# A feed-forward over four experts, computed by sorted slots of one expert each

## The chip, the cores and the metric

The kernel runs on one core of one Trainium2 chip. The metric is the device time of one execution in microseconds (us); the time given is the median of 3 runs.

## The reference

Two layers act on x of shape (2, 2048, 128), float32. Attention has 16 heads of width 8, a causal window of 128 tokens, and a latent branch over 64 pooled rows, mixed by a gate. It is kept as it is. The feed-forward picks one of four experts for each token:

```python
x = x + _layernorm(attention(_layernorm(x)))
x = x + _layernorm(ffn(_layernorm(x)))

# ffn, on x of 4096 tokens, H = 128, I = 512, E = 4
logits = x @ W_router
expert_idx = jnp.argmax(logits, axis=-1)
h = jnp.einsum('th,ehi->tei', x, W1) + b1
h = jax.nn.gelu(h, approximate=False)
onehot = jax.nn.one_hot(expert_idx, E, dtype=x.dtype)
intermediate = jnp.einsum('te,tei->ti', onehot, h)
y = intermediate @ Wo + bo + x
y = _layer_norm(y, ln_gamma, ln_beta)
```

## The kernel before

Tokens lie in 32 tiles of 128 (NB), which make 8 chunks of 512 (NCH, four tiles each, CT). The program has three parts, each a block that every engine leaves before the next begins.

`project` norms x, makes q, k and v and writes q and k to DRAM in three bfloat16 parts. `attend` goes over the tiles in steps s = -2 to 34 (`schedule`). In step s each engine does, in eight groups g = 0 to 7, a piece of the score maxima of tile s + 2, the probabilities and values of tile s, and the gate, output product and norming of tiles s - 1 to s - 3. So the last three steps, 32 to 34, only drain. The order on each engine is written out by hand: PE scores, products and transposes; DVE maxima (L1097) and small row operations, with `ystats`, `yve`, `ybias` for the norming of tile s - 3; ACT exponentials (L1325) and the norming `yn` (L1376); POOL the causal clearing of probabilities (L1242, L1245), the power `yrstd` (L1270), gate arithmetic, and last the addition of `yn` to X (L1311). In steps 30 and 31 DVE also splits the biases b1 into three bfloat16 parts (L1107 to L1125) and makes the low part of W1 (L1129). SP issues the loads. Where PE would pause, bfloat16 products of a constant tile fill the time (`keep_warm`, L124, and `beside`).

`InputNorm` norms the 512 rows of one chunk for the feed-forward: statistics and aggregate on DVE (L197, L201), epsilon and power on POOL (L206, L209), four subtract-and-multiply operations on DVE (L215).

`ffn` goes over the chunks, a straight start, a hardware loop and a straight end. A chunk is transposed (PE, L1531), split in a high and a low fp32r part, and its logits are made (L1542). DVE turns them into a one-hot row with five small operations (L1640 to L1650), which PE transposes and spreads over the partitions, one expert at a time (L1521). DVE multiplies the high and the low part by each expert's row (L1689, L1690), so that a token's columns are zero for three experts. PE then sums over all four experts for each quarter j of I:

```python
def hidden(c, j, e):
    for k, (w, x) in enumerate(((w1hi, xehi), (w1lo, xehi), (w1hi, xelo))):
        nc.tensor.matmul(psH[j % 2][:], w[:, e, tile], x[:, u, e], ...)
```

That is 48 matmuls of 512 columns in a chunk (L1510), and one for the bias of each quarter (L1513). ACT applies Gelu (L1769), PE multiplies by Wo (L1553, 16 matmuls that stand as 32 in the profile). The rest stands one and two chunks later: DVE adds the input (L1675), statistics (L1598, L1602), the norming (L1697); POOL gamma and beta (L1752, L1756); then DVE a second norming (L1610), the residual (L1615), and SP stores the chunk in one DMA (L1489).

## Time and profile before

| | |
|---|---|
| median of 3 runs | 551.62 us (549.55 to 555.9) |
| the profiled execution | 553.63 us |
| its span, first to last instruction | 551.8 us |
| mean granted TensorE clock | 0.955 |
| busy: PE, DVE, ACT, POOL | 506.1, 428.4, 297.2, 326.9 us |
| attention begins, ends | about 85, 367 us |
| feed-forward | 367 to 552 us |

Times in the profile count from the span's start. PE is the matmul engine and PEld its weight loads, DVE the vector, ACT the scalar, POOL the GpSimd engine, SP the one that issues DMAs here (SPq is its queue). A row names line, engine, operation, output<-inputs. A duration of an instruction runs from its start to its end and may overlap with the next one's, so the spacing of two starts is what one costs in a row.

### The profile page before, as it was taken

The numbers are of one execution on the slowest core, as the hardware profiler recorded it, in microseconds if no ns is written. First come the engines' busy times: TensorE is split into PE (matmuls) and PEld (weight loads), VectorE is DVE, ScalarE is ACT, GpSimd is POOL, SyncE is SP. The second block draws the span as 40 slices with busy tenths as digits, with TensorE's granted clock in tenths as the row PEclk, the third lists the DMA queues.
The fourth block names the chain that finished last, engine by engine and source line by source line (L and its number), as shares of the span: only waits on it lengthen the run. The fifth ranks groups of instructions, "written<-read, shape, count | busy, mean of one in ns | idle before, by whom it ended". The sixth has DMA issues, their size and how long they took to land. (4 is left out here: it accounts for less than half of the span.)

```text
span 551.8 us, 16727 instructions
## 1 busy us (share of the span) xinstructions
PE 506.1 (92%) x5277; PEld 312.0 (57%) x5280; DVE 428.4 (78%) x2018; ACT 297.2 (54%) x820; POOL 326.9 (59%) x735
## 2 busy tenths in 40 slices
PE   8978579999999999999999999869999999999991
PEld 3434224565666565565665665535677577677671
DVE  5986586899999999999999898635657677685655
ACT  2655305788888888788888888512211211312110
POOL 4799302688888888588888789841113333333241
PEclk9999855999999999999999999988999999999996
DMA  4465460324213323222332000000000000000001
GB/s 127 132 221 174 150 109 2 100 66 97 46 32 61 83 63 64 45 36 64 64 64 58 10 4 4 2 1 0 1 1 1 21 20 0 19 20 0 20 19 39
DMA packets 49059, 28.10 MB, mean 51 GB/s; under 512 B 6808, under 2 KB 48056, under 8 KB 48976
## 3 DMA queue, kind: packets, MB, share of 16 engines
q1 hardware_dynamic: 47648, 26.73, 19.7%
q8 instruction: 41, 0.67, 0.5%
q10 hardware_dynamic: 1328, 0.36, 0.3%
q14 instruction: 42, 0.34, 0.2%
HBM read 17.90 MB, written 8.91 MB: 49 GB/s over the span
## 5 line engine op out<-in xcount | busy, mean ns | idle before, releaser
L1097 DVE CUSTOM_DVE_ANT_0 added<-psS,maskq 128x256 bf16<-128x256 f32 x512 | 199.8, 415 | 25.4 <-PE psS L938 18.5
L1325 ACT ACTIVATE probs<-psST 128x512 f32<-128x512 f32 x240 | 143.4, 598 | 37.5 <-PE psST L974 35.3
L974 PE MATMUL psST<-qst,kst 50*128 50x128 bf16 x992 | 101.1, 222 | 0.0
L938 PE MATMUL psS<-kst,qst 48*128 48x256 bf16 x448 | 91.7, 287 | 2.3 <-DVE rowmax L1097 1.3
L1769 ACT ACTIVATE hT<-fpsH 128x512 f32<-128x512 f32 x32 | 19.2, 599 | 121.6 <-PE fpsH L1513 121.6
L995 PE MATMUL psPV<-probs,vst 128*10 128x128 f32 x1984 | 80.1, 277 | 3.1 <-issue 0.6
L1242 POOL TENSOR_SCALAR_AFFINE_SELECT probs<-probs 128x256 f32<-128x256 f32 x150 | 62.0, 414 | 5.2 <-ACT probs L1325 5.0
L1245 POOL TENSOR_SCALAR_AFFINE_SELECT probs<-probs 128x256 f32<-128x256 f32 x150 | 62.6, 417 | 0.0
L938 PEld LDWEIGHTS psS<-kst,qst 48*128 48x128 bf16 x448 | 25.2, 95 | 62.4 <-issue 39.5
L974 PEld LDWEIGHTS psST<-qst,kst 50*128 50x128 bf16 x992 | 55.9, 95 | 0.0
L1510 PE MATMUL fpsH<-xehi,w1hi 128*128 128x512 f32 x128 | 55.7, 435 | 0.0
L995 PEld LDWEIGHTS psPV<-probs,vst 128*10 128x10 f32 x1984 | 43.4, 91 | 16.0 <-issue 5.7
L1510 PE MATMUL fpsH<-xelo,w1hi 128*128 128x512 f32 x128 | 50.6, 395 | 0.0
L1510 PE MATMUL fpsH<-xehi,w1lo 128*128 128x512 f32 x128 | 50.5, 395 | 0.0
L1097 DVE DVE_READ_ACCUMULATOR2_ANT rowmax<- 128x1 f32 x512 | 42.6, 83 | 0.0
L962 PE MATMUL psST<-maskk,identb 128*128 128x512 bf16 (+1 forms) x106 | 40.1, 378 | 0.0
L1752 POOL TENSOR_TENSOR y<-y,gamma 128x512 f32<-128x512 f32 x7 | 9.1, 1293 | 52.1 <-DVE y L1697 52.1
L1364 ACT ACTIVATE lexp<-psA,lmin 128x64 f32<-128x64 f32 (+1 forms) x128 | 37.1, 300 | 0.0
L1689 DVE TENSOR_TENSOR xehi<-fpsE,xfThi 128x512 fp32r<-128x512 f32 x32 | 22.0, 688 | 19.3 <-PE fpsE L1521 9.7
L1553 PE MATMUL fpsY<-wo,hT 128*128 128x128 f32 x256 | 30.6, 278 | 0.7 <-ACT hT L1769 0.7
L1510 PEld LDWEIGHTS fpsH<-xehi,w1hi 128*128 128x128 f32 x128 | 24.0, 188 | 11.9 <-issue 8.4
L1553 PEld LDWEIGHTS fpsY<-wo,hT 128*128 128x128 f32 x256 | 29.2, 192 | 1.2 <-ACT hT L1769 1.0
(198 smaller groups left out, 1078.8 us busy)
## 6 DMA issues: line engine op xcount, KB each, us to landing
q_parts<-early SPq DMA_DIRECT2D x8, 384.0 KB, 2.6
k_parts<-early SPq DMA_DIRECT2D x8, 384.0 KB, 2.7
qst<-q_parts SPq DMA_DIRECT2D x32, 96.0 KB
kst<-k_parts SPq DMA_DIRECT2D x32, 96.0 KB
X<-in_L_attn_x_dram SPq DMA_DIRECT2D x8, 256.0 KB, 3.2
qst<-q_parts SPq DMA_DIRECT2D x32, 64.0 KB
kst<-k_parts SPq DMA_DIRECT2D x32, 64.0 KB
out_dram<-res SPq DMA_DIRECT2D x8, 256.0 KB, 2.3
```

The costliest lines, as they stand in the source:

```text
L938: last = nc.tensor.matmul(bank[:, a], q, kst[rows, slot, ring(n - 1, 2)], start=True, stop=True)
L962: nc.tensor.matmul(psST[g % 2][:].rearrange("p a (s q) -> p a s q", s=2)[:, :, sides[0]:2], identb[:], maskk[:, sides[0]:2].unsqueeze(1).b ...
L974: last = nc.tensor.matmul(bank[:, a, side * P:(side + 1) * P], kst[rows, slot, ring(n - 1 + side)], qst[rows, slot, ring(n)], start=not ma ...
L995: last = nc.tensor.matmul(psPV[32 * t:32 * t + VW, G * P:(G + 1) * P], vst[:, n.k - 1 + side, SLOTS * (t // 2) + 2 * G + a, :], probs[:, u ...
L1097: taken = nc.vector.tensor_tensor_reduce(added[:, 2 * (g % 2) + a], psS[g % 2][:, a], mask, 1.0, NEG * 4, ALU.add, ALU.max, rowmax[:, n.mo ...
L1242: nc.gpsimd.affine_select(out=before, in_=before, compare_op=ALU.is_gt, fill=0.0, base=0, pattern=[[0, 2], [1 - P, P]], channel_multiplier=P)
L1245: nc.gpsimd.affine_select(out=own, in_=own, compare_op=ALU.is_gt, fill=0.0, base=0, pattern=[[0, 2], [1, P]], channel_multiplier=-1).then_ ...
L1325: nc.scalar.activation(probs[:, g ^ 1], psST[g % 2][:].rearrange("p a c -> p (a c)"), ACT.Exp, scale=SCALE).then_inc(s_exp.sem, 1)
L1364: nc.scalar.activation(per_lat(lexp, s)[:, h], per_lat(psA, s)[:, h], ACT.Exp, bias=lmin[:, s.mod(2), h:h + 1], scale=-1.0, accum_out=lsum ...
L1510: nc.tensor.matmul(psH[j % 2][:], w[:, e, tile], x[:, u, e], start=(e == 0 and k == 0), stop=False)
L1553: last = nc.tensor.matmul(psY[:, t * P:(t + 1) * P], hT[:, m.mod(2), j, t * P:(t + 1) * P], wo[:, j], start=(j == 0), stop=(j == IT - 1))
L1689: nc.vector.tensor_tensor(xehi[:, u, e], psE[e % 2][:], xfThi[:, u].bitcast(F32), ALU.mult)
```

## The change

Each token goes through its own expert only. Three things are new.

First, routing. `Route` takes one chunk: four transposes and a copy (`turned`, `copied`), logits, the choice (six small DVE operations, now with a signed one-hot), ranks of the tokens among those of their expert (eight small bfloat16 matmuls with a triangle and with ones), places (five small DVE operations, with a running count `following`), and `move`: four indirect DMAs, issued on POOL, that scatter 128 rows of 1028 bytes each (normed row, row, token number) to a DRAM buffer `by_expert`. Chunks 0 to 4 are routed in steps 30 to 34 of attention, chunks 5 to 7 at the head of `ffn`. The buffer holds two pairs of experts, each filled from both ends, and is blanked before by 19 stores on ACT's queue in steps 3 to 21.

Second, slots. DVE maps 11 slots of 512 rows (8 + 4 - 1) to experts and places, 23 small operations. Slots beyond those used read a blank one, so 11 are always computed. SP reads expert and place of each slot into registers and loads the slot's rows and weights, six and three deep. PE does 12 expert matmuls of 512 columns for a slot instead of 48 for a chunk. The bias is added by Gelu.

Third, the steps of a slot stand over four iterations: PE transposes n + 1, multiplies n, and makes the output of n - 1. ACT does both normings, four operations each, with bias and scale tiles; DVE does gamma and beta and the sums; POOL the two powers and four indirect stores of 128 rows. The nine operations on b1 leave DVE. In steps 30 and 31 only two groups of eight keep their `beside` fillers. The first norming writes into a tile `rows`, which also holds the row itself in place of X. `project` gets some 37 small memsets and an iota.

```diff
+SLOT = CH
+NS = NCH + E - 1
+TILE_RING = 6
+W_RING = 3
+ROUTED = 5
+ROUTE_FROM = NB - 2
...
+    def turned(self, pe, c, bank):
+        nc, norm = self.nc, self.norm
+        pe.wait_ge(norm.s_xf.sem, norm.s_xf.after(c))
+        pe.wait_ge(self.s_rTc.sem, self.s_rTc.after(c - 1))
+        for t in range(CT):
+            last = nc.tensor.transpose(bank[:, t * P:(t + 1) * P], self.held.rows[:, c.times(CT, t), 0:D], self.ident[:])
+        last.then_inc(self.s_rT.sem, 1)
...
+    def logits(self, pe, c, bank):
+        u = c.mod(2)
+        pe.wait_ge(self.s_rTc.sem, self.s_rTc.after(c))
+        pe.wait_ge(self.s_place.sem, self.s_place.after(c - 1))
+        for t in range(CT):
+            last = self.nc.tensor.matmul(bank[:, t * E:(t + 1) * E], self.xfT[:, u, t * P:(t + 1) * P], self.held.wr[:],
+                                         start=True, stop=True)
+        last.then_inc(self.s_logit.sem, 1)
...
+    def ranks(self, pe, c, bank):
+        nc, ones = self.nc, self.filler[:, 0:P]
+        pe.wait_ge(self.s_oh.sem, self.s_oh.after(c))
+        pe.wait_ge(self.s_place.sem, self.s_place.after(c - 1))
+        flat = self.signed[:].rearrange("p t e -> p (t e)")
+        nc.tensor.matmul(bank[:, 0:CT * E], self.held.tri[:], flat, start=True, stop=False)
+        for t in range(1, CT):
+            nc.tensor.matmul(bank[:, t * E:CT * E], ones, flat[:, 0:(CT - t) * E], start=False, stop=(t == CT - 1))
+        for t in range(CT):
+            last = nc.tensor.matmul(bank[:, CT * E:(CT + 1) * E], ones, self.signed[:, t],
+                                    start=(t == 0), stop=(t == CT - 1))
+        last.then_inc(self.s_rank.sem, 1)
...
+    def move(self, pool, c):
+        if c.k == 0:
+            pool.wait_ge(self.s_blank, 16 * (SPARE + 1))
+        pool.wait_ge(self.s_place.sem, self.s_place.after(c))
+        pool.wait_ge(self.norm.s_xf.sem, self.norm.s_xf.after(c))
+        for t in range(c.times(CT), c.times(CT, CT)):
+            self.nc.gpsimd.indirect_dma_start(self.by_expert,
+                                              bass.IndirectOffsetOnAxis(ap=self.where[:, t:t + 1], axis=0),
+                                              self.held.rows[:, t], None, bounds_check=2 * PAIR_ROWS - 1,
+                                              oob_is_err=False).then_inc(self.s_moved, 16)
...
+        def routed(s, lead=0):
+
+            c = s.k - ROUTE_FROM + lead
+            return chunk(c) if 0 <= c < ROUTED + lead else None
...
+                            if not (s + 2).live and g in (0, 6):
+                                beside(bankT, g % 2, 2 * P)
...
+                    if g == 2 and routed(s):
+                        route.turned(pe, routed(s), bankT)
+                    if g == 4 and routed(s):
+                        route.logits(pe, routed(s), bankR)
+                    if g == 6 and routed(s):
+                        route.ranks(pe, routed(s), bankP)
...
+                    if (g, a) == (0, 1) and routed(s, 1):
+                        c = routed(s, 1)
+                        dve.wait_ge(s_x1.sem, s_x1.after(step(0, CT * c.k + CT - 1)))
+                        norm.statistics(dve, c)
+                    if (g, a) == (1, 0) and routed(s):
+                        norm.apply(dve, routed(s))
+                    if (g, a) == (5, 1) and routed(s):
+                        route.choose(dve, routed(s), bankR)
+                    if (g, a) == (7, 1) and routed(s):
+                        route.places(dve, routed(s), bankP)
...
+                if routed(s, 1):
+                    norm.deviations(pool, routed(s, 1))
...
+                if routed(s):
+                    route.move(pool, routed(s))
...
+                    if g == 7 and 3 <= s.k < 3 + SPARE + 1:
+                        block = s.k - 3
+                        act.dma_start(by_expert[block * SLOT:(block + 1) * SLOT].rearrange("(t p) w -> p t w", p=P),
+                                      held.blank[:].unsqueeze(1).broadcast_to([P, CT, ROW])).then_inc(s_blank, 16)
...
+            sp.wait_ge(s_map, MAPPED)
+            for i in range(W_RING):
+                load_weights(i)
...
+            sp.wait_ge(route.s_moved, 16 * NB)
+            for i in range(W_RING):
+                load_tile(i)
+            for i in range(W_RING, NS):
+                load_tile(i)
+                load_weights(i)
...
+            for c in range(ROUTED, NCH):
+                route.ranks(pe, chunk(c), psP[:])
+                if c + 1 < NCH:
+                    route.turned(pe, chunk(c + 1), psT[0][:])
+                    route.logits(pe, chunk(c + 1), psR[:])
+                keep_warm(nc, psY[1][:], filler, 5)
+            keep_warm(nc, psY[1][:], filler, 24)
...
-                for k, (w, x) in enumerate(((w1hi, xehi), (w1lo, xehi), (w1hi, xelo))):
-                    nc.tensor.matmul(psH[j % 2][:], w[:, e, tile], x[:, u, e], start=(e == 0 and k == 0),
-                                     stop=False)
-                if e == E - 1:
-                    nc.tensor.matmul(psH[j % 2][:], b1p[:, j * P:(j + 1) * P], onehotT[:, u], start=False,
-                                     stop=True).then_inc(s_h.sem, 1)
...
+                for k, (w, x) in enumerate(((0, xhi), (1, xhi), (0, xlo))):
+                    last = nc.tensor.matmul(psH[j % 2][:], w1[:, r, w, cols], x[:, u], start=(k == 0), stop=(k == 2))
+                last.then_inc(s_h.sem, 1)
...
+            for i in range(-1, NS + 1):
+                n = nth_slot(i)
+                if (n + 1).live:
+                    transposed(n + 1)
                 if n.live:
...
+                    hidden(n, 0)
+                    hidden(n, 1)
+                if (n - 1).live:
+                    outputs(n - 1)
...
                 if n.live:
...
+                    hidden(n, 2)
+                    hidden(n, 3)
...
+            norm.apply(dve, chunk(ROUTED))
+            for c in range(ROUTED, NCH):
+                route.choose(dve, chunk(c), psR[:])
+                if c + 1 < NCH:
+                    norm.statistics(dve, chunk(c + 1))
+                route.places(dve, chunk(c), psP[:])
+                if c + 1 < NCH:
+                    norm.apply(dve, chunk(c + 1))
...
+            for i in range(-1, NS + 3):
+                n = nth_slot(i)
+                if (n - 3).live:
+                    shift(s_sh3, s_rs3, n - 3, mv3, rstd3, shift3)
+                if (n + 1).live:
+                    low(n + 1)
+                if (n - 2).live:
+                    shift(s_sh2, s_rs2, n - 2, mv2, rstd2, shift2)
+                if (n - 3).live:
+                    result(n - 3)
+                if (n - 2).live:
+                    affine(n - 2)
+                if (n - 1).live:
+                    summed(n - 1)
...
+            def normed(n):
+                u = n.mod(2)
+                act.wait_ge(s_sh2.sem, s_sh2.after(n))
+                act.wait_ge(s_y4.sem, s_y4.after(n - 2, 1))
+                for t in range(CT):
+                    last = nc.scalar.activation(y2[:, u, t], y1[:, u, t], ACT.Identity, bias=shift2[:, u, t:t + 1],
+                                                scale=rstd2[:, u, t:t + 1])
+                last.then_inc(s_y2.sem, 1)
...
+            for i in range(0, NS + 3):
+                n = nth_slot(i)
+                if (n - 2).live:
+                    deviations(s_st2, s_rs2, s_y2, n - 2, ve2, rstd2)
+                if (n - 3).live:
+                    store(n - 3, range(CT - 1))
+                if (n - 2).live:
+                    deviations(s_st3, s_rs3, s_y5, n - 2, ve3, rstd3)
+                if (n - 3).live:
+                    store(n - 3, range(CT - 1, CT))
```

On POOL, the drain of attention, steps 32 to 34. Names: `yrstd` the power for a tile's norming, `gdiff`, `mixed` and `diff` the gate, `X` or `rows` the residual row, `rstd` the power of `InputNorm`. Before:

```order
L1270 TENSOR_TENSOR yrstd<-yve,mhalf 128x1
L1280 TENSOR_TENSOR gdiff<-diff,gate 128x128
L1285 TENSOR_TENSOR mixed<-gdiff,both 128x128
L1297 TENSOR_TENSOR diff<-both 128x144
L1311 TENSOR_TENSOR X<-X,yn 128x128
L206 TENSOR_TENSOR ve<-mv,eps_col 128x4
L209 TENSOR_TENSOR rstd<-ve,mhalf 128x4
L1270 TENSOR_TENSOR yrstd<-yve,mhalf 128x1
```

And after the change, from the end of step 31:

```order
L1449 TENSOR_TENSOR rows<-X,yn 128x128
L297 DMA by_expert<-rows,where 9728x257 x4
L334 TENSOR_TENSOR rstd<-ve,mhalf 128x4
L1408 TENSOR_TENSOR yrstd<-yve,mhalf 128x1
L1418 TENSOR_TENSOR gdiff<-diff,gate 128x128
L1423 TENSOR_TENSOR mixed<-gdiff,both 128x128
L1435 TENSOR_TENSOR diff<-both 128x144
L1449 TENSOR_TENSOR rows<-X,yn 128x128
L297 DMA by_expert<-rows,where 9728x257 x4
L334 TENSOR_TENSOR rstd<-ve,mhalf 128x4
L1408 TENSOR_TENSOR yrstd<-yve,mhalf 128x1
```

Four indirect DMAs and the power of the next chunk now stand between a step's residual row and the next step's `yrstd`.

On ACT, one chunk of the feed-forward's straight start before. `xfT` and `xfThi` are the transposed chunk and its high part, `onehotT` the choice, `hT` the Gelu:

```order
L1777 ACTIVATE xfT<-fpsT 128x512
L1779 ACTIVATE xfThi<-xfT 128x512
L1769 ACTIVATE hT<-fpsH 128x512 x2
L1786 ACTIVATE onehotT<-fpsO 12x512
L1769 ACTIVATE hT<-fpsH 128x512 x2
```

And one slot after (L1944 is the second norming, of slot n - 3, L1935 the first, of n - 2):

```order
L1921 ACTIVATE xhi<-fpsT 128x512
L1944 ACTIVATE y<-y,shift,rstd 128x128 x4
L1927 ACTIVATE hT<-fpsH,bias 128x512 x2
L1935 ACTIVATE y<-y,shift,rstd 128x128 x4
L1927 ACTIVATE hT<-fpsH,bias 128x512 x2
```

The two normings, DVE's before, stand ahead of and between the Gelus.

On DVE, one slot after. `xlo` is the low part, `shift` minus mean times the power, `res` the row to be stored:

```order
L1820 SCALAR_TENSOR_TENSOR shift<-mv,rstd 128x4
L1826 TENSOR_TENSOR xlo<-fpsT,xhi 128x512
L1820 SCALAR_TENSOR_TENSOR shift<-mv,rstd 128x4
L1845 TENSOR_TENSOR res<-y,tile 128x512
L1831 TENSOR_TENSOR y<-y,gamma 128x512
L1835 TENSOR_TENSOR y<-y,beta 128x512
L1809 BN_STATS fstats<-y 128x6 x4
L1813 BN_AGGR mv<-fstats 128x2 x4
L1815 TENSOR_SCALAR ve<-mv 128x4
L1851 TENSOR_TENSOR y<-fpsY,tile 128x512
L1855 TENSOR_TENSOR y<-y,bob 128x512
L1809 BN_STATS fstats<-y 128x6 x4
```

The affine part of slot n - 2, which waits for ACT's norming, stands ahead of the sum of slot n - 1, whose output PE has made.

## Rows read from the trace of the kernel before

**Rows 1.** Busy time by stage: length, PE, PEld, DVE, ACT, POOL, granted clock, DMA share, GB/s.
```profile
85.00:366.00 281.00, 268.83 (x4113) 162.90 (x4113) 248.51 (x1383) 228.48 (x705) 223.78 (x585) 0.97 0.22 47
...
409.00:540.00 131.00, 130.22 (x670) 92.16 (x667) 85.85 (x300) 25.32 (x43) 44.80 (x54) 1.00 0.05 15
```

**Rows 2.** The chain that ended last, one chunk: start, length, what.
```profile
457.95 0.59 PE fpsT L1531 x4
458.54 2.80 PE fpsH L1510 x12
...
461.66 0.98 PE fpsR L1542 x8
462.64 3.68 PE fpsY L1553 x32
```

**Rows 3.** Groups by line and form: busy us, mean ns of one, idle before.
```profile
L1675 DVE TENSOR_TENSOR y<-fpsY,XF 128x512 f32<-128x512 f32 x8 | 5.5, 690 | 5.5 <-PE fpsY L1553 5.5
...
L1729 POOL TENSOR_TENSOR rstd<-ve,mhalf 128x4 f32<-128x4 f32 x16 | 16.2, 1014 | 1.3
...
L1769 ACT ACTIVATE hT<-fpsH 128x512 f32<-128x512 f32 x32 | 19.2, 599 | 121.6 <-PE fpsH L1513 121.6
...
L1376 ACT ACTIVATE yn<-y,ybias,yrstd 128x128 f32<-128x128 f32 x32 | 16.0, 501 | 4.2 <-DVE ybias L1164 4.2
...
L654 ACT ACTIVATE early<-psQ,bq 128x512 bf16<-128x512 f32 x8 | 5.5, 684 | 7.8 <-DMA rq_t<-early 6.5 <-PE psQ L706 1.3
```

**Rows 4.** DVE in order of time: start, length, operation, idle time before it.
```profile
372.30 0.17 DVE L1642 TENSOR_TENSOR iseq<-fpsR,lmx 128x16 f32<-128x16 f32 x1
372.50 0.17 DVE L1645 TENSOR_TENSOR rank<-iseq,prio 128x16 f32<-128x16 f32 x1
...
447.08 0.87 DVE L1598 BATCH_NORM_STATS2 fstats<-y 128x6 f32<-128x128 f32 x4
448.11 0.38 DVE L1602 BATCH_NORM_AGGREGATE mv<-fstats 128x2 f32<-128x6 f32 x4 [0.15 <-DVE fstats L1598]
449.70 1.12 DVE L1610 TENSOR_SCALAR y<-y,mv,rstd 128x128 f32<-128x128 f32 x4 [1.22 <-POOL rstd L1729]
```

**Rows 5.** POOL in order of time, steps 30 and 31.
```profile
343.27 0.94 POOL L1242 TENSOR_SCALAR_AFFINE_SELECT probs<-probs 128x256 f32<-128x256 f32 x1
...
352.69 0.41 POOL L1245 TENSOR_SCALAR_AFFINE_SELECT probs<-probs 128x256 f32<-128x256 f32 x1
```

**Rows 6.** All engines in order of time, from attention into the feed-forward.
```profile
357.43 3.19 PE L124 MATMUL psS<-filler 128*128 128x512 bf16 x14
...
362.83 0.46 POOL L1311 TENSOR_TENSOR X<-X,yn 128x128 f32<-128x128 f32 x1 [2.40 <-ACT yn L1376]
...
366.38 0.45 POOL L1311 TENSOR_TENSOR X<-X,yn 128x128 f32<-128x128 f32 x1 [1.32 <-ACT yn L1376]
367.62 1.27 POOL L1739 TENSOR_TENSOR XF<-xf,bob 128x512 f32<-128x512 f32 x1 [0.79 <-DVEq L130]
...
368.26 0.63 PE L1531 MATMUL fpsT<-ident,xf 128*128 128x128 f32 x4 [4.22 <-issue]
```

**Rows 7.** SP's queue in order of time: issues of DMAs.
```profile
0.94 6.48 SPq L428 DMA_DIRECT2D X<-in_L_attn_x_dram  x3
...
149.76 0.30 SPq L231 DMA_DIRECT2D kst<-k_parts  x1
```

**Rows 8.** DMA issues: count, KB each, median us from issue to landing.
```profile
q_parts<-early SPq DMA_DIRECT2D x8, 384.0 KB, 2.6
...
out_dram<-res SPq DMA_DIRECT2D x8, 256.0 KB, 2.3
```

**Rows 9.** Busy time in stretches of 3 us, columns as in rows 1.
```profile
369.00:372.00 3.00, 3.00 (x13) 2.30 (x12) 0.00 (x0) 1.16 (x2) 0.00 (x0) 0.50 0.00 0
...
540.00:543.00 3.00, 0.00 (x0) 0.00 (x0) 2.58 (x11) 0.00 (x0) 0.45 (x2) 0.98 0.01 3
543.00:546.00 3.00, 0.00 (x0) 0.00 (x0) 2.62 (x11) 0.00 (x0) 0.76 (x1) 0.50 0.00 0
```

781 lines of the change are left out of this document (398 added, 383 removed).

## The prediction

> **What bounds the kernel now.** I read first the busy time by stages [rows 1]. Attention (85 to 366 us) has PE busy 269 of 281 us, with DVE, ACT and POOL each at 224 to 249: four engines near their limit. The feed-forward loop (409 to 540) has PE busy 130.2 of 131 us and DVE only 86: PE alone bounds it. Behind it comes an epilogue of 12 us without PE. Then the chain of waits in the loop [rows 2]: it is PE from end to end. In a chunk of 20.2 us (the transposes recur at 437.74 and 457.95) 48 expert matmuls stand 2.80/12 = 0.233 us apart, and the output product takes 3.68. So work that computes four experts for each token and keeps one is what PE is busy with, and taking it away must pay on PE. The question is what is late next. For that I read the lengths and spacings of the small operations [rows 3, 4], POOL at attention's end [rows 5], the step from one part to the next [rows 6], and the DMA rows [rows 7, 8].
>
> **The slots: period.** PE issues per slot 4 transposes (0.59), 12 expert matmuls (2.80) and the output product (3.68): 7.1 us [rows 2]. Eleven slots make 78 us where eight chunks took about 160. But the engines wait for each other in a ring, as the order on ACT shows: second norming of slot n-3, two Gelus of n, first norming of n-2, and DVE's affine part of n-2 stands ahead of its sum of n-1. One turn, from the end of DVE's statistics to the next:
> - shift of slot n-3 on DVE 0.16, its hand-over 0.05;
> - four ACT normings with scale and bias read from tiles: 0.50 long [rows 3], about 0.10 overlapping with the next: 4 x 0.41 + 0.10 = 1.74. The trace has no four in a row: bounds 0.25 each (half the length) and 0.50;
> - two Gelus, now with a bias tile: a biased 512-wide activation is 0.68 long against 0.60 [rows 3]; 2 x 0.58 = 1.16;
> - four ACT normings of slot n-2: 1.74, hand-over 0.05;
> - DVE gamma and beta: 0.69 + 0.04 each [rows 3], 1.46; statistics: 0.87, aggregate from 1.03 to 1.41 after the start [rows 4], epsilon 0.2: 1.65. Together 3.11;
> - DVE sum of output, of bob and statistics: again 3.11.
> Sum 11.1; by writing the turn out event by event, with low parts and POOL beside it, I get 10.9 a slot. POOL has 2 x 1.01 for the powers [rows 3] and four indirect stores; these lie beside it as long as a store issues in under 1.6 us. Ring: first tile landed to end of slot 0's sum 14.1; ten turns 106.4; then affine 6.8, power, shift, norming and residual 3.7, four stores 4.0 and a landing of about 2 (2.3 for a store of 256 KB [rows 8]): 137.1 us.
>
> **An indirect DMA on POOL** appears 76 times and never in the trace. A plain issue on SP takes 0.30 us; the first three loads of x took 6.48/3 = 2.2 each [rows 7]. POOL's own routine on four numbers takes 1.01 [rows 3]. I take 1.0, nearest to what POOL does by program, and keep 0.3 and 2.2 for the range. POOL's work is stretched beside some of DVE's: the same select is 0.41 in one place and 0.94 in another [rows 5]. The Trainium skill ("SBUF — State Buffer", SBUF: two separate sides) warns that descriptor generation on GpSimd cannot write its descriptors while VectorE is in a two-port mode, about 620 ns alone and 3100 ns beside such a copy. The trace has no such DMA to test it; the stretched selects are of that family. By 3.1 us POOL would need over 14 us a slot. That is rival C below, priced there from rows.
>
> **Attention's last steps.** In steps 30 and 31 POOL was already full (its rows stand end to end from the select at 343.27 to the last one at 352.69 [rows 5]). It gets three powers (3.0) and the four moves of chunk 0 (4.0); nine b1 operations leave DVE, whose neighbourhood stretched POOL's selects, worth about 2.5. So step 31 ends 4.5 us later: its last select ends at 357.6, not 353.1. In steps 32 to 34 each engine must pass a routing in place: statistics 1.65, norming 1.1, four transposes 0.6, copy 0.6, logits 1.0, six choice operations at 0.207 spacing 1.25, ranks 0.8, five place operations 1.05 [rows 2, 4], hand-overs 0.4: 8.5 us, where the last additions to x stand 3.6 us apart (362.83 and 366.38 [rows 6]). Behind the moves on POOL stands the next step's power and yrstd (1.0 + 0.55), for which DVE's ybias waits ahead of its choice. In step 33 the 14 to 15 fillers (3.19 [rows 6]) stand ahead of the ranks on PE. Walking these orders: POOL is free of chunk 1's moves at 362; places of chunk 2 end at 370.3, of chunk 3 at 383.1, of chunk 4 at 392.7; its four moves end at 396.7. Before, POOL's last addition ended at 366.8 and the next part began 0.8 later [rows 6]. Attention ends 29.9 us later, of which 25.4 belong to the drain. The same 0.8 gives 397.5 for the next part's start. The 16 fillers beside the scores that go run beside other matmuls: nothing.
>
> **Blank stores and memsets.** 19 stores of 0.5 MB from ACT's queue, an issue each of 0.3 us against ACT's 52 us of idle time in attention [rows 1, 7]: 1 us, at worst 8. Some 37 tiny memsets before the first statistics hide partly behind the fillers: 0.5. The four b1 loads go through queues with slack: 0.
>
> **Head of the feed-forward.** Three chunks are routed with nothing beside them, since norming c+1 stands on DVE behind placing c. Per chunk: norming 1.1, transposes 0.7, copy 0.65, logits 1.5 (at the half clock that PE is granted after such a pause [rows 9]), choice 1.25, statistics of the next 1.65 (over the ranks), places 1.05, hand-overs 0.15: 8.0; the last without statistics 7.2. Sum 23.2. POOL's moves (4.0) lie beside. Then 23 dependent small operations at 0.2 [rows 4] make the map: 4.5. SP issues six weight loads (0.3 each [rows 7]) after three register loads, whose price the trace does not show (bounds 0.2, a small operation, and 1.0, POOL's power; I take 0.6), and waits for the last moves, which land 4.0 + 2 after the places: the first tile's load is issued 4.5 + 1.8 + 1.8 + 0.4 = 8.5 after the places. Its 0.5 MB stand behind weights of 1.5 MB; 384 KB land in 2.6 [rows 8], so I take 4. First tile at 12.5.
>
> **Sum.** Against the profiled execution (span 551.8, its time 553.6; the median of the runs is 551.6): 1.5 + 397.5 + 23.2 + 12.5 + 137.1 + 0.5 for the end = 572.3, 20.5 above the span. The feed-forward alone shrinks from 184.2 (367.6 to 551.8) to 173.8, and attention and start give 31 back. On the median: 551.6 + 20.5 = 572, rounded.
>
> **Rivals.** A, faster: the ring does not form. If ACT's normings overlap to 0.25 each and the hand-overs vanish, DVE is the bound: 2 x 3.11 + low parts and residual 1.2 + shifts 0.3 = 7.8 a slot, 3.1 less than 10.9. Ten turns give 31 back: 541. It decides below 9 us a slot. For it: DVE and ACT are both under 8 us of work. Against it: the order on ACT is fixed, and the normings are 0.50 long [rows 3]. B, no change: the ring at 0.33 a norming gives 7 back and issues at 0.5 us on POOL another 8 (2 in each of four places): 557; with a little more of either, 552. C, POOL: an indirect DMA takes 2.2. Then the four sets of moves on the path, 4.8 each, give 19, and POOL's slot is 2.0 + 8.8 and more with waits, 14 in place of 10.9 only if its order bites; I count 1.2 a slot: 572 + 19 + 12 = 603. D, PE's clock: PE idles about 3.1 us in one piece in each turn. Rows 9 show the grant at 1.00 or 0.98 (2.4 GHz) in the first 3 us without PE work and at 0.50 (1.2 GHz) in the next 3, and at 0.50 when PE resumed after 4.2 us. The Trainium skill ("TensorE: Matmul & The Clock Gate", Part 1: The HAM clock gate) says that an idle stretch returns the clock to half; the trace agrees after 4.2 us [rows 6, 9] and leaves 3.1 open. At half speed PE needs 14.2 us a slot (7.1 doubled), 3.3 above the ring: 572 + 36 = 608 if in all slots, some 584 if in a third.
>
> **Chances and range.** Forecast (slower, 562 to 585): 0.50. A 0.10, with milder forms of it that end below 546: 0.13 together. B 0.12. C 0.15, D 0.10. A measurement here tells about 1% from no change: faster 0.13, within 1% 0.12, slower 0.75. The range for 8 in 10 takes in B's upper half, C and most of D: 550 to 604; the forecast's own is 560 to 586.
>
> **What would show it.** Right: PE at some 65% in the slots with ACT's first norming waiting for its shift, and DVE's gamma operation waiting for ACT; 10.5 to 11.5 us between output products; attention's last POOL work near 397; a lone routing of 8 us a chunk in the head; 12 us between the last place and the first transposed tile. Wrong: output products under 9 us apart (A); POOL busy without a gap, its issue over 1.6 us (C); a granted clock of 0.50 inside slots with expert matmuls 0.43 apart (D); attention ending before 380, if moves cost nearly nothing or the drain's waits overlap more than I walked.

## The result and the profile after

The changed kernel takes 600.05 us (median of 4 runs, 599.25 to 601.93), the kernel before 550.59 beside it (4 runs, 549.12 to 555.9): a ratio of 1.088, 95% interval 1.081 to 1.096. It is slower, as forecast, but by 49 us and not by 20. In the profiled execution the span is 597.5 us, 45.7 above the 551.8 of before. The forecast for this span was 572.3.

Where the 25 us beyond the forecast lie can be read by setting the points of my sum beside the trace:

| | before | forecast | after | beyond |
|---|---|---|---|---|
| step 31's last select ends | 353.1 | 357.6 | 366.6 | 9.0 |
| attention's last POOL work ends | 366.8 | 396.7 | 411.45 | 5.8 |
| the next part's first operation | 367.6 | +0.8 | 415.78 (+4.3) | 3.5 |
| last place, after that | | 23.2 | 25.7 | 2.5 |
| first transposed tile, after that | | 12.5 | 15.7 (457.14) | 3.2 |
| slots and end, after that | | 137.6 | 140.4 | 2.8 |

The sum of the last column is 26.8; the 1.5 us that I gave to attention's start (blank stores, memsets) did not come, which leaves 25.3.

Each row is read from a time line. First POOL from the end of step 30 into step 31 (compare [rows 5] and [rows 6]); columns are start, length, operation, and in brackets the idle time before it and what ended it:

```profile
350.96 0.45 POOL L1449 TENSOR_TENSOR rows<-X,yn 128x128 f32<-128x128 f32 x1
352.47 1.19 POOL L297 DMA_INDIRECT by_expert<-rows,where  x1 [1.06 <-issue]
353.96 0.97 POOL L297 DMA_INDIRECT by_expert<-rows,where  x1 [0.31 <-issue]
355.23 0.97 POOL L297 DMA_INDIRECT by_expert<-rows,where  x1 [0.30 <-ACT probs L1465]
356.50 0.97 POOL L297 DMA_INDIRECT by_expert<-rows,where  x1 [0.30 <-issue]
357.49 1.07 POOL L334 TENSOR_TENSOR rstd<-ve,mhalf 128x4 f32<-128x4 f32 x1
358.52 0.55 POOL L1408 TENSOR_TENSOR yrstd<-yve,mhalf 128x1 f32<-128x1 f32 x1
...
366.60 0.45 POOL L1449 TENSOR_TENSOR rows<-X,yn 128x128 f32<-128x128 f32 x1
```

Here stands the operation that the trace of before didn't show. An indirect DMA of 128 rows holds POOL for 0.97 us, and the next starts 1.27 after it: my 1.0 was right for its length, but 0.30 of issue belongs to each, and the first of a group costs 1 us more. Four take 6.1 us from the addition, not 4.0. Before, the `yrstd` of this step stood right behind the addition:

```profile
344.54 0.89 POOL L1311 TENSOR_TENSOR X<-X,yn 128x128 f32<-128x128 f32 x1
345.40 0.99 POOL L1270 TENSOR_TENSOR yrstd<-yve,mhalf 128x1 f32<-128x1 f32 x1
```

In steps 29 and 30 of the changed kernel there are no moves, but the new power waits for the statistics on DVE (`ve`):

```profile
328.27 1.01 POOL L334 TENSOR_TENSOR rstd<-ve,mhalf 128x4 f32<-128x4 f32 x1 [1.56 <-DVE ve L327]
...
339.51 1.57 POOL L334 TENSOR_TENSOR rstd<-ve,mhalf 128x4 f32<-128x4 f32 x1 [1.04 <-DVE ve L327]
```

Behind the moves stand two powers, and behind these DVE:

```profile
359.10 0.41 DVE L1302 SCALAR_TENSOR_TENSOR ybias<-ymv,yrstd 128x1 f32<-128x1 f32 x1 [4.11 <-POOL yrstd L1408]
...
374.41 0.36 DVE L1302 SCALAR_TENSOR_TENSOR ybias<-ymv,yrstd 128x1 f32<-128x1 f32 x1 [3.79 <-POOL yrstd L1408]
...
387.97 0.36 DVE L1302 SCALAR_TENSOR_TENSOR ybias<-ymv,yrstd 128x1 f32<-128x1 f32 x1 [4.03 <-POOL yrstd L1408]
...
402.98 0.16 DVE L1302 SCALAR_TENSOR_TENSOR ybias<-ymv,yrstd 128x1 f32<-128x1 f32 x1 [4.11 <-POOL yrstd L1408]
```

Four steps, four waits of 4 us: the wait that the prediction named, in every step. Its length isn't its price. In steps 33 and 34 the logits, which DVE needs next, end on PE only 0.3 and 0.4 us before this wait does (at 387.66 and 402.59), so that without the moves DVE would wait for PE there almost as long. PE's time line of step 33 shows the fillers, 14 in 5.65 us where [rows 6] had 14 in 3.19; the granted clock was 0.50 (1.2 GHz) over the whole of 375 to 390, where these fillers had 1.00 (2.4 GHz) before:

```profile
387.90 5.65 PE L139 MATMUL psST<-filler 128*128 128x512 bf16 x14 [0.24 <-issue]
393.39 0.27 PE L1218 MATMUL psB<-ident,mixed 128*128 128x128 f32 x1
```

The transposition of `mixed` stands behind them. Then the step from one part to the next, POOL's last work and DVE's first:

```profile
410.47 0.98 POOL L297 DMA_INDIRECT by_expert<-rows,where  x1 [0.30 <-issue]
415.78 1.12 DVE L340 TENSOR_SCALAR rows<-rows,mv,rstd 128x128 f32<-128x128 f32 x4 [10.01 <-PEq L899]
```

For 4.3 us the profile shows no engine at work; before it was 0.8 [rows 6]. SP's queue shows the way to the first tile, after the last place at 441.47 and the end of the map at 445.8:

```profile
446.80 0.59 SPq L1640 DMA_DIRECT2D w1s<-w1hi  x1
447.53 0.53 SPq L1640 DMA_DIRECT2D w1s<-w1lo  x1
449.09 0.50 SPq L1640 DMA_DIRECT2D w1s<-w1hi  x1
...
451.80 0.53 SPq L1640 DMA_DIRECT2D w1s<-w1lo  x1
453.40 3.91 SPq L1649 DMA_DIRECT2D tile<-by_expert  x4
```

POOL had issued the last move at 446.1, so the tiles wait for SP: three pairs of weights recur every 2.2 us (an issue of 0.5 to 0.6 each and a register load of about 1.0).

Last the slots. The chain of waits in one turn (start, length, what) is the ring of the prediction, operation by operation:

```profile
504.54 1.25 ACT y L1944 x3
505.78 1.15 ACT hT L1927 x2
506.93 1.55 ACT y L1935 x4
508.51 0.70 DVE y L1831
509.23 0.70 DVE y L1835
509.96 0.89 DVE fstats L1809 x4
...
511.79 0.69 DVE y L1851
512.51 0.70 DVE y L1855
513.23 0.88 DVE fstats L1809 x4
...
515.33 1.25 ACT y L1944 x3
```

A turn took 10.5 us in the middle (six turns between the residuals at 495.34 and 558.53), against 10.9 forecast. The groups say the same (busy us, mean ns of one | idle before): ACT's second norming waits for DVE's shift, DVE's gamma for ACT's first norming, and a norming is 0.48 long, 0.39 apart:

```profile
L1887 POOL DMA_INDIRECT out_dram<-res,tile x44 | 47.2, 1073 | 32.6 <-DVE res L1845 23.7 <-issue 9.0
...
L1944 ACT ACTIVATE y<-y,shift,rstd 128x128 f32<-128x128 f32 x44 | 18.1, 482 | 50.9 <-DVE shift L1820 50.9
L1935 ACT ACTIVATE y<-y,shift,rstd 128x128 f32<-128x128 f32 x44 | 18.0, 483 | 0.5 <-DVE shift L1820 0.5
...
L1831 DVE TENSOR_TENSOR y<-y,gamma 128x512 f32<-128x512 f32 x11 | 7.6, 693 | 19.4 <-ACT y L1935 19.4
```

By stages, as [rows 1] (length, PE, PEld, DVE, ACT, POOL, granted clock):

```profile
85.00:366.00 281.00, 267.35 (x4055) 163.28 (x4054) 245.21 (x1385) 227.10 (x697) 219.84 (x576) 0.95 0.34 85
484.00:568.00 84.00, 60.09 (x374) 51.39 (x372) 55.21 (x206) 46.75 (x103) 51.80 (x49) 0.94 0.27 86
```

In the slots no engine is above 72%: everybody waits in turn.

### The profile page after: what moved, and what is told of

It is laid out like the page before. It is cut to its first block and busy times, and to the rows that moved or that the text cites. A ratio compares the mean times of both kernels' runs of the same rounds, so it can differ in the third digit from the quotient of the medians.

```text
span 597.5 us, 16735 instructions
## 1 busy us (share of the span) xinstructions
PE 467.3 (78%) x5123; PEld 295.5 (49%) x5127; DVE 421.1 (70%) x2132; ACT 336.5 (56%) x914; POOL 377.5 (63%) x772
## 5 line engine op out<-in xcount | busy, mean ns | idle before, releaser
L1124 PE MATMUL psST<-qst,kst 50*128 50x128 bf16 x992 | 102.5, 224 | 0.0
L1145 PE MATMUL psPV<-probs,vst 128*10 128x128 f32 x1984 | 82.5, 283 | 6.2 <-issue 2.3
L1887 POOL DMA_INDIRECT out_dram<-res,tile x44 | 47.2, 1073 | 32.6 <-DVE res L1845 23.7
L1896 POOL TENSOR_TENSOR rstd<-ve,mhalf 128x4 f32<-128x4 f32 x22 | 22.9, 1039 | 42.9 <-DVE ve L1815 42.8
L1697 PE MATMUL fpsH<-xhi,w1s 128*128 128x512 f32 x88 | 32.0, 447 | 19.6 <-ACT hT L1927 19.5
L1944 ACT ACTIVATE y<-y,shift,rstd 128x128 f32<-128x128 f32 x44 | 18.1, 482 | 50.9 <-DVE shift L1820 50.9
L297 POOL DMA_INDIRECT by_expert<-rows,where x32 | 31.9, 998 | 20.8 <-DVE where L289 11.5
L1706 PEld LDWEIGHTS fpsY<-wo,hT 128*128 128x128 f32 x352 | 43.1, 200 | 2.7 <-ACT hT L1927 1.9
L1706 PE MATMUL fpsY<-wo,hT 128*128 128x128 f32 x352 | 43.3, 284 | 1.2 <-ACT hT L1927 1.2
L1927 ACT ACTIVATE hT<-fpsH,bias 128x512 f32<-128x512 f32 x44 | 28.1, 676 | 6.0 <-PE fpsH L1697 5.9
L1435 POOL TENSOR_TENSOR diff<-both 128x144 f32<-128x144 f32 x32 | 15.7, 490 | 22.8 <-DVE both L1344 22.8
```

What stands on the lines that cost most here:

```text
L297: self.nc.gpsimd.indirect_dma_start(self.by_expert, bass.IndirectOffsetOnAxis(ap=self.where[:, t:t + 1], axis=0), self.held.rows[:, t], No ...
L1124: last = nc.tensor.matmul(bank[:, a, side * P:(side + 1) * P], kst[rows, slot, ring(n - 1 + side)], qst[rows, slot, ring(n)], start=not ma ...
L1145: last = nc.tensor.matmul(psPV[32 * t:32 * t + VW, G * P:(G + 1) * P], vst[:, n.k - 1 + side, SLOTS * (t // 2) + 2 * G + a, :], probs[:, u ...
L1706: last = nc.tensor.matmul(psY[u][:, t * P:(t + 1) * P], hT[:, u, j, t * P:(t + 1) * P], wo[:, j], start=(j == 0), stop=(j == IT - 1))
L1887: nc.gpsimd.indirect_dma_start(out_rows, bass.IndirectOffsetOnAxis(ap=tile[:, r, t, 2 * D:ROW].bitcast(U32), axis=0), res[:, u, t], None, ...
L1927: nc.scalar.activation(hT[:, n.mod(2), j], psH[j % 2][:], ACT.Gelu, bias=bias[:, (E - 1) % 2, n.k, j:j + 1]).then_inc(s_gelu.sem, 1)
```

## The experiments

Spans are of the profiled execution; the changed kernel's is 597.5. Ratios are to the kernel before, run beside each.

How far two executions differ can be read here. Seven of these kernels (the changed one, no_fillers, last_move_in_head, tiles_early, sum_first, orders_6 and orders_8) run the same code up to step 31, and that step's addition begins at 366.60, 366.62, 368.08, 366.00, 369.93, 368.02 and 369.49 in them. So a difference of up to 4 us between two spans, or between two of these additions, doesn't show by itself what an edit did. Smaller gains below are read from the spacing of the rows around the edit.

**Is a routing cheaper in attention than at the head?** In `all_at_head`:

```diff
-ROUTED = 5
+ROUTED = 0
```

> No chunk is routed in attention; all eight are routed at the head of the feed-forward, where one takes 8.8 us (norming at 415.78, 424.58 and 433.38 in the changed kernel). Theory 1, the five routings in attention each cost about as much as they would at the head, because the drain waits for them in a row: attention ends near 368 again (one more statistics: up to 371), the part after it begins 0.8 to 1 us later since no indirect DMA stands near its end, the head takes 8 x 8.8 = 70 us: last place at 439 to 442 against 441.5, span 595 to 598, no change. Theory 2, routing beside attention's last steps hides most of it and only the block exit and the drain's waits were mispriced: then taking it out must lose: 5 x 8.8 = 44 us more at the head against less than 35 saved, span 607 or more. The 4.3 us between POOL's last indirect DMA and the next part's first operation: if they belong to the indirect DMAs, the gap is 0.8 to 1 here; if they belong to the larger program, it stays above 4.

Span 594.9, ratio 1.079 (1.073 to 1.084). Attention's last addition is at 366.07 as before the change (366.38), the next part begins 1.1 us after it ends, and the last place is at 437.2, 69.6 later: 8.7 a chunk. Theory 1 held: five routings in attention cost 48 us there (3 of them the later start of the next part), 44 at the head. Also seen: the 19 blank stores, the memsets and the b1 operations that went are worth nothing in sum. Steps 30 and 31, which hold no routing here, last 9.27 and 8.48 us where they lasted 10.07 and 8.52: 0.8 at most for the b1 operations.

```profile
366.07 0.45 POOL L1449 TENSOR_TENSOR rows<-X,yn 128x128 f32<-128x128 f32 x1 [0.80 <-ACT yn L1521]
...
367.62 1.12 DVE L340 TENSOR_SCALAR rows<-rows,mv,rstd 128x128 f32<-128x128 f32 x4 [2.15 <-PEq L899]
```

**The moves.** In `moves_late` the routing stays in attention, and POOL issues all moves at the head:

```diff
-                if routed(s):
-                    route.move(pool, routed(s))
...
-            for c in range(ROUTED, NCH):
-                if c + 1 < NCH:
-                    norm.deviations(pool, chunk(c + 1))
+            for c in range(NCH):
                 route.move(pool, chunk(c))
+                if ROUTED + c + 1 < NCH:
+                    norm.deviations(pool, chunk(ROUTED + c + 1))
```

> The indirect DMAs of all chunks are issued at the head of the feed-forward, none in attention; the routing itself stays where it is. Theory 1, the moves on POOL are what DVE's ybias waits for (3.8 to 4.1 us in each of four steps): attention ends 4 x 5 = 20 us earlier, near 391, and the next part begins about 1 us later, at 392 in place of 415.8; the last place is at 418; POOL then needs 8 x 5.1 = 41 us for the moves, so that they end near 434 and the first tile's transposes come near 441 to 444 (457.1 before): span 581 to 585. Theory 2, the drain is bound by the routing's own passes through PE, ACT and DVE: attention ends only 4 to 8 us earlier (about 405), and since the moves then end at 448 and the tiles come after, span 593 to 600.

Span 600.5. Neither theory was right in full. Step 31's addition came at 362.60 in place of 366.60 and the last at 395.38 in place of 403.74, 8.4 us sooner. But the places of chunk 4 end only at 399.4, and the next part began at 404.27. PE had new work on the path: the 14 fillers of step 33 again (5.5 us, POOL waits 9.04 behind them), and the 11 at the end. At the head the moves of eight chunks then make a chain of 48 us on POOL.

`no_fillers` is the changed kernel without the fillers of step 33 (15 in the code) and the 11 at the end, `moves_late_no_fillers` is moves_late without them. (Both expectations count 15 in step 34 as well; the condition around them is met in step 33 only.)

```diff
-                            keep_warm(nc, last_bank, filler, 15)
+                            keep_warm(nc, last_bank, filler, 0)
...
-            keep_warm(nc, last_bank, filler, 11)
+            keep_warm(nc, last_bank, filler, 0)
```

> The changed kernel without the fillers of attention's last steps (15 each in steps 33 and 34, 11 at the end). Theory 1, in step 33 PE was granted half its clock, so 14 fillers take 5.65 us where 3.19 were counted, and POOL's last additions and the places wait for what stands behind them: without them the last moves end 5 us sooner, span 592; the 11 at the end lie beside POOL's moves and give nothing. Theory 2, the drain is bound by POOL (moves and powers) and the fillers are hidden: within 1 us of 597.5. Theory 3, fewer fillers leave PE cold for longer: span above 599.

> The moves of all chunks at the head as in moves_late (600.5), and no fillers in the last steps. There PE's fillers held the output product back by 5.5 us (POOL's addition waited 9.04 for yn) and the 11 at the end (4.6 us) stood between the last ranks and the block's exit. Theory 1: both are on the path once the moves are gone: attention ends 10 us sooner, the next part begins near 394 in place of 404.3, its POOL ends its moves 48 us later as there, span 590. If it is the routing's own passes that bind: 597 or more. The gap from the last work to the next part's first operation was 1.1 there and 4.3 with moves at the end: 1.1 again.

Spans 594.1 and 596.2, 3.4 and 4.3 less than with them. That is within the spread, but the step shows it: in the first, step 33 took 12.3 us (additions at 377.84 and 390.15) in place of 16.6. Fillers that hid something at 2.4 GHz are work on the path at 1.2. The forecasts of 592 and 590 were too good: in the second, step 31 took 14.9 us in place of 12.0 (additions at 351.82 and 366.72), with PE granted 0.50 from 345 to 360. Up to there its code is that of moves_late, so the edit didn't cause this, and the 4 us that moves_late gained at step 31 don't show in this kernel.

**Which part of a full step's routing made step 31 late?** The three variants are beside fillers in five groups of eight (`more_beside`), fillers in the pauses themselves (`warm_pauses`), and one routing less in the full steps (`four_routed`).

```diff
-                            if not (s + 2).live and g in (0, 6):
-                                beside(bankT, g % 2, 2 * P)
+                            if not (s + 2).live and g in (0, 1, 5, 6, 7):
+                                beside(bankT, 0, 2 * P)
```

> The changed kernel with beside fillers in five of eight groups in steps 30 and 31 in place of two (the groups in which the bank is free). In the changed kernel PE was granted 1.00 up to 345 us and 0.50 to 0.52 from 345 to 354, where the kernel before had 1.00 with fillers in all groups; PE was busy 3.0 of 3 us at half clock. Theory 1, the fillers taken away let the clock fall, and that is why step 31 ends 9 us later than forecast: with them the clock stays near 1.00 there, step 31's last select comes near 361 in place of 366.2, span 591 to 593. Theory 2, the waits for the routing make the pauses, which fillers that are issued only at fixed places in the order don't fill: clock as before, and the added fillers cost 0 to 3 us: 597 to 601.

Span 596.9; clock 0.50 from 345 to 360, step 31's addition at 367.90. Theory 2: these fillers don't hold the clock.

```diff
+                            keep_warm(nc, bankT, filler, 3)
                         route.turned(pe, routed(s), bankT)
...
+                            keep_warm(nc, psS[1][:].rearrange("p a k -> p (a k)"), filler, 4)
                         values(s, 0)
...
+                            keep_warm(nc, psS[1][:].rearrange("p a k -> p (a k)"), filler, 3)
                         route.logits(pe, routed(s), bankR)
```

> The changed kernel with bfloat16 fillers (three, four, three) put where PE waits in steps 30 and 31: ahead of the routing's transposes, of the first values and of the logits. more_beside left the clock at 0.50 from 345 to 360, since its fillers stand beside scores and not where PE pauses. Theory 1, the pauses of 1 to 2 us in step 30 (PE busy 1.86 of 3 us at 342 to 345) let the clock fall, and half the clock in step 31 is what makes it late: with fillers in the pauses the clock stays at 1.00 up to 354, step 31's addition comes near 361 in place of 366.6, span 592 to 594. Theory 2, the routing's chain through DVE, ACT, PE and POOL sets the step's length whatever the clock: addition at 365 to 369, span 596 to 600.

Span 599.1. The stretch from 345 to 357 in this kernel, with the columns of [rows 1]:

```profile
345.00:357.00 12.00, 11.45 (x147) 7.42 (x147) 6.96 (x35) 7.76 (x23) 8.74 (x17) 1.00 0.07 25
```

In the changed kernel PE was granted 0.57 there:

```profile
345.00:357.00 12.00, 12.00 (x111) 7.38 (x110) 5.82 (x33) 6.57 (x20) 7.87 (x15) 0.57 0.10 33
```

The clock was held at 2.4 GHz in this stretch, and the addition comes at 369.92, later still. But the stretch is step 30 and the first third of step 31. Step 30 took 13.1 us in place of 13.7. From 357 to 360 PE was busy for 0.35 us, and from 360 to 372 it was granted 0.50, so the rest of step 31 ran at half clock here too. The gain of theory 1 didn't come, but this run alone can't say what half the clock costs in step 31; the split of the steps behind the next variant does.

```diff
-ROUTED = 5
-ROUTE_FROM = NB - 2
+ROUTED = 4
+ROUTE_FROM = NB - 1
```

> Chunk 0 is routed in step 31, and only four chunks in attention (steps 31 to 34); the fourth to the head, where one takes 8.8 us. The forecast gave steps 30 and 31 only what stands on POOL (powers, moves) and nothing for the passes of a routing through PE, ACT and DVE. If a routing in a full step costs as much as one in the drain (9 to 10 us): step 31's addition comes 6 to 9 us sooner, near 358 to 360, attention ends near 402, the head is 8.8 longer, span 596 to 598, no change. If only the waits for the moves of chunk 0 made step 31 late: addition at 362.6, attention ends 407, span 601 to 602.

Span 595.4. Step 31's addition is at 357.10: one routing less in the full steps, with its statistics and moves, is worth 9.5 us. That is as much as the mean of the five (48/5 = 9.6) or one at the head (8.8). Its last move ends at 401.5, and the fourth chunk at the head gives the gain back, as expected.

The steps can be split at POOL's `yrstd`. Ahead of it stand what follows the last addition: moves, the new power and its wait. Behind it stands the step's old work up to its own addition. In us, for steps 29, 30 and 31, from the starts of these rows:

| | ahead of `yrstd` | behind it |
|---|---|---|
| before | 1.33, 1.75, 0.86 | 7.13, 8.32, 7.66 |
| changed kernel | 3.80, 3.83, 7.56 | 7.97, 9.90, 8.08 |
| all_at_head | 3.80, 1.62, 0.62 | 8.06, 7.65, 7.86 |
| four_routed | 1.33, 3.91, 3.09 | 7.05, 8.21, 7.61 |
| moves_late | 3.79, 3.82, 3.92 | 6.76, 10.78, 8.05 |
| moves_late_no_fillers | 3.79, 3.92, 3.91 | 8.02, 10.52, 10.99 |
| warm_pauses | 3.80, 3.83, 7.19 | 7.96, 9.29, 11.04 |

The changed kernel is 14.1 us longer than before over these steps, and 11.3 of it stand ahead of `yrstd`, where POOL works or waits for DVE's `ve`. (The 7.56 is 7.56 to 7.58 in five kernels with the same code.) The moves account for 3.6 (7.56 against 3.92), less than their 6.1, since the wait for `ve` runs beside them. The powers with their waits account for 7.6. The other 2.8 stand behind `yrstd`: what half the clock and the routing's pass through the engines cost in these steps, less the 0.8 or so of the b1 operations. Half the clock may cost more: moves_late and moves_late_no_fillers have the same code up to here, and behind `yrstd` step 31 took 8.05 with a grant of 1.00 and 10.99 with 0.50 up to 360 us.

**The 4.3 us at the end of attention.** `last_move_in_head` issues only chunk 4's moves at the head:

```diff
-                if routed(s):
+                if routed(s) and routed(s).k < ROUTED - 1:
                     route.move(pool, routed(s))
...
+                if c == ROUTED:
+                    route.move(pool, chunk(c - 1))
                 route.move(pool, chunk(c))
```

> Only the moves of chunk 4 go from the end of attention to the head of the feed-forward, where POOL has gaps. In the changed kernel the next part began 4.3 us after POOL's last indirect DMA, where it begins 1.1 after the last work in kernels without moves in attention. Theory 1, the gap is the time that the block's exit waits for an engine whose last work was an indirect DMA: here POOL's last work in attention is a small addition, PE's 11 fillers after the last ranks (405.0 + 4.6) end last, and the next part begins 1.1 later, near 410.8: 5 us gained, span 592.5. Theory 2, any indirect DMA in the block makes its exit long (a queue to be emptied or its descriptors): 409.6 + 4.3 = 413.9, span 595.6.

PE's last filler ends at 410.05, the next part begins at 411.09, 1.04 later: theory 2, a longer exit whatever stands last, fell. all_at_head, moves_late and this kernel, whose POOL does not end on moves, have gaps of 1.0 to 1.1; those that did (no_fillers 407.53 to 412.02, tiles_early, four_routed, the changed kernel) 3.4 to 4.5. Of the 4.7 us won, 2.8 reach the end (span 594.7).

What the exit waits for stays open. The last indirect DMA of attention ended at 402.02 here, so a wait of some 4.4 us behind it, whatever POOL does after, would have been over at 406.4 and would not show either. And its length seems to go with the number of such DMAs in the block. Attention was left 4.1 to 4.5 us after the last of 20, and 3.4 after the last of 16 (four_routed). The program ends 4.8 us after the last store where its last part holds 56 (eight kernels), 5.2 where it holds 60 (four_routed and this one), and 6.5 where it holds 76 (all_at_head, both moves_late and both piped_head kernels). No experiment was made on this.

**The first tile.** `tiles_early`:

```diff
-            for i in range(W_RING):
-                load_weights(i)
+            load_weights(0)
             sp.wait_ge(route.s_moved, 16 * NB)
             for i in range(W_RING):
                 load_tile(i)
+                if i:
+                    load_weights(i)
```

> SP loads one slot's weights, then waits for the moves and issues the first tile, and the other weights after it; before, it issued six weight loads with three register reads (446.8 to 452.3) ahead of the first tile at 453.4, while the moves had been issued at 447.07. If SP's issues and register reads are what made the first tile late (15.7 us after the places, 12.5 forecast): the first tile's load is issued near 449.5 and the first transposes start at 453.2, 4 us sooner, span 593.5. If the landing of the moves is what it waits for: first tile issued after 451, span 595 to 597.5.

The first tile is issued at 448.37, 8.2 us after the last place, and transposed at 452.10, 12.0 after it: 3.7 less than in the changed kernel, as forecast. Span 592.9.

**The ring.** `sum_first` changes one order on DVE:

```diff
+                if (n - 1).live:
+                    summed(n - 1)
                 if (n - 2).live:
                     affine(n - 2)
-                if (n - 1).live:
-                    summed(n - 1)
```

`orders_6` and `orders_8` change three orders, on DVE, POOL and ACT, with six and eight tiles:

```diff
-TILE_RING = 6
+TILE_RING = 8
...
+                if (n - 2).live:
+                    shift(s_sh2, s_rs2, n - 2, mv2, rstd2, shift2)
+                if (n + 1).live:
+                    low(n + 1)
+                if (n - 3).live:
+                    shift(s_sh3, s_rs3, n - 3, mv3, rstd3, shift3)
+                if (n - 1).live:
+                    summed(n - 1)
+                if (n - 2).live:
+                    affine(n - 2)
+                if (n - 3).live:
+                    result(n - 3)
...
+                if (n - 1).live:
+                    deviations(s_st2, s_rs2, s_y2, n - 1, ve2, rstd2)
+                if (n - 2).live:
+                    deviations(s_st3, s_rs3, s_y5, n - 2, ve3, rstd3)
+                if (n - 3).live:
+                    store(n - 3, range(CT))
...
                 if (n - 2).live:
                     normed(n - 2)
+                if (n - 3).live:
+                    normed_again(n - 3)
```

> In each slot's turn DVE does the sum of slot n - 1 ahead of the affine part of slot n - 2, nothing else is changed. If the ring through DVE alone sets the 10.47 us of a turn (shift, four normings, two Gelus, four normings, affine, sum), DVE works while ACT norms, and a turn falls to about 8 us: ten turns give 24 back, span 573. If other waits stand close behind (POOL takes the power of the first norming behind stores and the power of the second, and a slot's tile is loaded only once the store six slots before has landed), a turn stays at 10.1 to 10.5 us and the span within 3 us of 597.5. My walk of the orders says the second: 10.1.

> The three new orders of orders_8 (578.4, a turn of 7.9 us), but with the six tiles of the changed kernel. If only the orders matter: 578 to 580 again. If the load of a tile, which waits for the landed store of the slot six before it, closes a second ring: the walk of the orders gives 11 us a turn, which is longer than the 10.47 of the changed kernel, and a span of 603 to 606.

> Three orders of the slots are changed together, with eight tiles in place of six: DVE sum before affine before residual, POOL the two powers next to each other ahead of all four stores, ACT two Gelus, first norming, second norming, two Gelus. The walk of the orders with the trace's durations gives 8.2 us a turn (DVE's work is 7.7, POOL's four issues of 1.33 and two powers of 1.02 are 7.4) and 15 us less in all: span 582. If PE's clock falls in its pauses or POOL's issues stretch beside DVE, a turn stays above 9 us and the span above 588.

| | turn, us | span |
|---|---|---|
| changed kernel | 10.5 | 597.5 |
| sum_first | 10.4 | 603.5 |
| orders_6 | 7.6 and 17.5 to 19 in turn | 609.5 |
| orders_8 | 7.9 | 578.4 |

(sum_first's first tile came 3.7 us later than the changed kernel's, at 460.80, before any slot; from there to the end it took 142.7 us against 140.4.) orders_6 shows the second ring that was expected, but a longer one: 13 us a turn in the mean, not 11. The swap alone opens one ring, and the next one holds: in sum_first POOL has the first norming's power behind a store and the power of the second, and DVE waits for it:

```profile
530.48 0.16 DVE L1820 SCALAR_TENSOR_TENSOR shift<-mv,rstd 128x4 f32<-128x4 f32 x1 [1.16 <-POOL rstd L1896]
...
532.79 0.16 DVE L1820 SCALAR_TENSOR_TENSOR shift<-mv,rstd 128x4 f32<-128x4 f32 x1 [1.55 <-POOL rstd L1896]
```

The three orders with six tiles run into the second ring, a tile that is loaded only when the store six slots before has landed, with PE waiting every other slot:

```profile
504.48 1.12 PE L1685 MATMUL fpsT<-ident,tile 128*128 128x128 f32 x4 [9.14 <-DMA tile<-by_expert]
...
531.07 1.11 PE L1685 MATMUL fpsT<-ident,tile 128*128 128x128 f32 x4 [10.25 <-DMA tile<-by_expert]
```

Eight tiles take that away, and PE, DVE and POOL are busy for 84 to 88% of the time. The busy times of 500 to 530 in orders_8, and behind them those of the changed kernel:

```profile
500.00:530.00 30.00, 26.39 (x180) 23.24 (x179) 26.48 (x100) 23.53 (x51) 25.14 (x24) 1.00 0.41 133
```

```profile
500.00:530.00 30.00, 20.04 (x137) 17.09 (x135) 19.55 (x75) 16.57 (x37) 18.06 (x18) 1.00 0.37 116
```

orders_8 is at 1.050 (1.044 to 1.056), 19 us under the changed kernel, and 21 (119.4 against 140.4) from the first tile on. Its turn of 7.9 is the 7.8 at which rival A put the bound of DVE.

**A version with the causes mended.** `piped_head` takes orders_8, no routing in attention, and overlaps the routings at the head; three chunks are normed in steps 29 to 34, and Gelu's table is loaded early:

```diff
+            for c in range(2):
+                route.turned(pe, chunk(c), psT[0][:])
+                route.logits(pe, chunk(c), psH[c % 2][:])
+            for c in range(NCH):
+                route.ranks(pe, chunk(c), psP[:])
+                if c + 2 < NCH:
+                    route.turned(pe, chunk(c + 2), psT[0][:])
+                    keep_warm(nc, psY[1][:], filler, 3)
+                    route.logits(pe, chunk(c + 2), psH[c % 2][:])
+                keep_warm(nc, psY[1][:], filler, 3)
```

> No chunk routed in attention; three chunks are only normed there (statistics in steps 29, 31, 33). At the head the routings overlap: PE transposes and makes the logits of chunk c + 2 while DVE chooses and places c; slots as in orders_8. By the runs so far: attention ends near 368 (366.5 in all_at_head; two more normings, 1 to 2), the head is bound by POOL, 5.1 us of moves and 1.04 of a power for each chunk, 8 x 5.1 + 5 x 1.04 = 46 us after the first place at 375: last moves at 421, landed at 423; first tile 4 later, 427; the slots and the end then took 119.4 in orders_8 (459.0 to 578.4): span 546 to 549. Rival: the engines' hand-overs and PE's half clock keep a chunk at 8.8 us in the head: last place at 439, span 567 to 570.

The second version:

```diff
             route.logits(pe, chunk(0), psH[0][:])
             for c in range(NCH):
                 route.ranks(pe, chunk(c), psP[:])
+                if c == 0:
+                    route.turned(pe, chunk(1), psT[0][:])
+                    route.logits(pe, chunk(1), psH[1][:])
...
                 load_tile(i, early[i])
+            load_weights(2)
```

> piped_head (550.7) with two edits: PE makes chunk 0's ranks ahead of chunk 1's transposes and logits (1.9 us of logits at half clock stood before them, and POOL's chain of moves starts with chunk 0's places): 1.2 us; and SP reads the three places and issues the tiles behind two weight pairs, not three (POOL's last move ended 421.4, the first tile was issued only at 425.99): 2 to 3 us. The head is a chain on POOL and the slots a chain behind the first tile, so both come through: span 547 to 548, 0.5 to 0.7% below the kernel before. If POOL's chain doesn't start earlier or the tile waits for the landing: 549.5 to 551.

piped_head: 552.74 us (10 runs), ratio 1.001 (0.999 to 1.003), span 550.7; the last move ends at 421.4 as forecast, the first tile is transposed at 429.94 and not 427. piped_head_2: ratio 1.001 (0.999 to 1.002), span 550.9; its first tile came 1.5 us sooner (428.49), and the slots lost it again by one turn of 8.9 us in which DVE waited 1.22 for PE's output product. Both reach the kernel before and neither beats it, against forecasts of 546 to 549 and 547 to 548. Of piped_head's miss 2.9 us are the first tile; 1.4 are slots and end, which took 120.8 and not the 119.4 of orders_8, since the program ends 6.5 us after its last store and not 4.8.

## Why the prediction was right in sign and wrong in size

- **The slots' ring** (10.9 a turn): the mechanism was right, and 10.5 was measured. PE was granted 1.00 from 470 to 530, but 0.85 from 540 to 550 and 0.66 from 560 to 570; the turns stayed at 10.5, so D's pauses came in part and its price did not. (Of the 4.2 us pause in [rows 6] D says that PE resumed at 0.50. Its first four transposes took 0.63 us there, as at full speed, and the clock fell 0.6 us later.) The total, 140.4 against 137.6, is close in part by luck: to the end of slot 0's sum 16.9 and not 14.1 (a table load of 1.28 on ACT and a grant of 0.73 from 458 to 470 stand in it), the ten turns 102.5 and not 106.4, and the rest 21.0 and not 17.0, of which 4.8 lie behind the last store where I had 2.5.
- **"An indirect DMA on POOL taken 1.0":** a term that was mis-sized. It is 0.97 to 1.07 long in most cases, but 1.27 from one to the next, and 1 more for the first of a group: 5.1 to 6.1 for four, not 4.0. Rival C (2.2) was too much; it lands near the measured time (603) by another mechanism, so its number is no success.
- **"So step 31 ends 4.5 us later":** the step that failed most; it ends 13.5 later. The forecast added what stands on POOL in steps 30 and 31, three powers (3.0) and four moves (4.0), and took off 2.5 for the b1 operations. It gave nothing to the waits ahead of the powers and to the routing's pass through PE, DVE and ACT. Steps 29, 30 and 31 last 11.8, 13.7 and 15.6 us where they lasted 8.5, 10.1 and 8.5: 3.3 + 3.7 + 7.1 = 14.1. By the split above, 7.6 of it are the powers, which wait for the statistics on DVE (1.56 and 1.04 in steps 29 and 30, the first a step earlier than I looked), 3.6 the moves, near the 4.0 forecast, and 2.8 what stands behind, where I had a gain. Of the gain of 2.5 at most 0.8 shows (all_at_head). How the 2.8 divide between the half clock and the routing's pass stays open.
- **"The 16 fillers beside the scores that go: nothing":** wrong in reason, and no run shows the effect alone. The clock fell to 0.57 from 345 to 357, and fillers beside the scores did not bring it back (more_beside). What it cost in this kernel is within the 2.8 above; with the clock at 1.00 step 30 was 0.6 shorter (warm_pauses).
- **Drain, 39.1 forecast, 44.9:** the waits were the ones named. Against the walk the trace falls behind by 1.3 us up to the places of chunk 2, by 2.2 more up to those of chunk 3, by 0.6 more up to those of chunk 4, and by 1.7 in the last four moves (5.7 and not 4.0). The 2.2 stand in the step of the fillers, which took 2.5 more at the half clock; I had written them down at 3.19 although PE pauses there.
- **"The same 0.8 gives the next part's start":** wrong, 4.3, behind POOL's last indirect DMA (last_move_in_head took it down to 1.0).
- **Head, 8.0 a chunk; 12.5 to the first tile:** 8.8, transposes at 1.11 and logits at 1.86 each at half the clock; and 15.7, as SP's register loads cost about 1.0 and not 0.6, and three pairs of weights stood ahead of the tiles (tiles_early: 12.0).
- **Blank stores and memsets (1.5):** nothing; the addition of step 28 came 0.55 us sooner than before (325.46 against 326.01).
- **The arithmetic:** the feed-forward's terms add up to 173.3 and not 173.8, and ten turns of 10.9 are 109 and not 106.4. Both are small beside the misses. The range for 8 in 10 (550 to 604) holds the result by the share that it took from C and D, and neither happened as described.

With all this the change could win only by what it takes from PE, and it does: from the first tile the slots need 140 us at a ring of 10.5, 119 at one of 7.9. But between attention's old end (367.6) and the first tile lie 90 us in the changed kernel and 62 in piped_head, a chain of small operations, waits and POOL's issues in which PE does no expert's product. Before, the first expert matmul stood at 381.05, 13 us into the feed-forward.

## What to carry to other kernels

When a small serial job is put into full steps, count its pass through every engine and what stands behind each of its waits, not only its busy time: here it cost as much inside the pipeline as alone (9.5, 9.6 and 8.8 us a chunk), and the waits ahead of its small operations count with it. An engine that issues software DMAs should have nothing behind them that others wait for, and its last DMA should stand some us ahead of a block's end. Before a small difference is explained, look at how far the same code differs between executions: here 4 us at step 31. Where all engines are between 55 and 72% in a loop, walk the orders to find the ring, and walk them again with the mend in place: one swap alone gained nothing, three together with a deeper buffer took 25% off a turn, and without the buffer made it longer.

## What the runs showed of the hardware

- An indirect DMA of 128 rows of 1028 bytes: 0.97 us of POOL, the next 1.27 after it, the first up to 1.06 later than its inputs. Beside DVE's operations on two tiles (gamma, beta or `bob`) in the slots some took 1.30 to 1.43. The Trainium skill ("SBUF — State Buffer", SBUF: two separate sides) warns of descriptor writes held up beside a two-port copy, to 3100 ns; the longest here are 0.4 us above the usual. None of these DVE operations is a copy, so the runs don't test the warning.
- A block whose last work is an indirect DMA is left 3.4 to 4.5 us after it, one that ends on other work 0.8 to 1.1. The program's end lies 4.8, 5.2 or 6.5 us behind the last of 56, 60 or 76 such DMAs in its last block. The reason is not shown.
- PE's grant can differ between two executions of the same code: from 354 to 360 us it was 1.00 in moves_late and 0.50 in moves_late_no_fillers, and step 31 took 2.9 us longer.
- The first Gelu of the slots loads a table for 1.28 us; in piped_head a dummy Gelu ahead of it let it load at 405.42, far ahead of the first slot.
